# A two-layer graph network on one core: one gathered tile of each round fetched as 128 one-row DMAs

## The reference

```python
h = x @ W
e = leaky_relu(a_src[src] + a_dst[dst], NEG_SLOPE)      # layer 0, self loops included
m = segment_max(e, dst); e = exp(e - m[dst]); denom = segment_sum(e, dst)
out = segment_sum(h[src] * (e / (denom[dst] + 1e-16))[:, None], dst)
x = layernorm(x + tanh(out + bias))
...
h = gelu(x @ W_pre + b_pre)                              # layer 1
aggr = segment_sum(h[src] * edge_attr, dst)
y = gelu(gelu((x + aggr) @ W1 + b1) @ W2 + b2)
x = layernorm(x + (x + aggr) + y)
```

## Time and profile before

| | |
|---|---|
| median of 3 runs | 3728.23 us (3727.25 to 3732.05) |
| the profiled execution | 3727.72 us, its span 3725.9 us |
| busy: POOL, DVE, PE, ACT | 2784.2, 2436.9, 2399.7, 1285.1 us |
| gathers from the tables into `rows` (L699) | 2850, 946 ns each, some 0.30 us of idle before each |
| granted clock of PE | 0.5 in layer 0, 0.9 in layer 1 |

### The profile page before, as it was taken

How to read it: one execution, slowest core, us unless ns; L and a number is a source line. 1 busy time by engine, 2 the same in 40 slices (tenths; PEclk the granted TensorE clock), 3 DMA queues, 4 the chain that set the end, 5 groups by cost and what they waited for, 6 DMA issues and landing times.

```text
span 3725.9 us, 65212 instructions
## 1 busy us (share of the span) xinstructions
PE 2399.7 (64%) x16704; PEld 1951.8 (52%) x16705; DVE 2436.9 (65%) x6240; ACT 1285.1 (34%) x3893; POOL 2784.2 (75%) x2950
## 2 busy tenths in 40 slices
PE   6433343434344444444445989989988989999888
PEld 3333333333333333333334777777776777777776
DVE  7544444444466666566666777777777778888886
ACT  5433343434445555555553111111111122111222
POOL 7777777777777777777775777777777777777776
PEclk7555555555555555555556999999999999999998
DMA  5222222222222222222223343443434343444443
GB/s 101 44 42 42 42 44 42 44 42 43 42 44 43 44 43 44 43 44 45 44 44 101 90 94 90 95 94 93 95 91 95 92 96 91 97 97 96 92 96 70
DMA packets 336816, 254.46 MB, mean 68 GB/s; under 512 B 239277, under 2 KB 264370, under 8 KB 336539
## 3 DMA queue, kind: packets, MB, share of 16 engines
q0 software_dynamic: 94016, 146.16, 19.5%
q1 hardware_dynamic: 227905, 99.65, 11.4%
q10 hardware_dynamic: 14618, 6.14, 0.6%
HBM read 244.43 MB, written 7.25 MB: 68 GB/s over the span
## 4 chain that ended last, share of the span: by engine, by line
POOL 52%; issue 22%; PE 10%; DVE 6%; ACT 5%; DMA 2%; ACTq 1%; DVEq 1%; POOLq 0%; SPq 0%
POOL rows L699 52%; PE bank L1136 8%; ACT onehot L796 2%; PE bank L1123 2%; DMA rows<-table,src_i 2%; DVE hot L1555 1%; DVE score L1411 1%; ACT L839 1%; ACT pair L816 1%; ACTq L788 0%; DVEq L1326 0%; DVE cand L1376 0%; DVE newp L1402 0%; DVE cand L1375 0%; ACTq L827 0%
## 5 line engine op out<-in xcount | busy, mean ns | idle before, releaser
L699 POOL DMA_INDIRECT rows<-table,src_i x2850 | 2697.5, 946 | 896.4 <-issue 853.2
L1136 PE MATMUL bank<-node,hot 128*128 128x288 bf16 x9310 | 1231.2, 295 | 28.8 <-issue 14.5
L1045 PE MATMUL bank<-onehot,rows 128*97 128x72 f32 (+1 forms) x3048 | 584.9, 369 | 789.8 <-ACT onehot L826 789.8
L1136 PEld LDWEIGHTS bank<-node,hot 128*128 128x128 bf16 x9310 | 932.0, 101 | 285.5 <-issue 17.9
L1045 PEld LDWEIGHTS bank<-onehot,rows 128*97 128x97 f32 x3048 | 530.8, 281 | 829.2 <-issue 767.1
L1555 DVE TENSOR_SCALAR hot<-node,key 128x642 bf16<-128x642 int16 x1862 | 870.2, 538 | 110.7 <-PE bank L1136 58.4
L950 ACT ACTIVATE pair<-dst_i 128x8 f32 (+1 forms) x196 | 35.2, 180 | 1183.2 <-DVE rows L1581 921.6
L796 ACT ACTIVATE onehot<-iota,far_dst 128x72 f32 (+1 forms) x1564 | 384.3, 328 | 23.2 <-ACT far_dst L793 0.4
L1389 DVE SCALAR_TENSOR_TENSOR other<-onehot,bank 128x576 f32<-128x576 f32 (+1 forms) x196 | 121.6, 621 | 397.8 <-ACT bank L809 307.3
L1123 PE MATMUL bank<-onehot,rows 128*96 128x40 f32 (+1 forms) x3128 | 305.7, 255 | 85.9 <-DVE acc L1591 42.5
L1123 PEld LDWEIGHTS bank<-onehot,rows 128*96 128x96 f32 x3128 | 294.2, 169 | 108.8 <-issue 78.1
(11 more groups left out here) (204 smaller groups left out, 1972.3 us busy)
## 6 DMA issues: line engine op xcount, KB each, us to landing
attr<-in_edge_attr_dram SPq DMA_DIRECT2D x190, 336.0 KB
rows<-table,src_i POOLq DMA_INDIRECT x2850, 2.5
node<-in_src_dram SPq DMA_DIRECT2D x39, 320.0 KB
attr<-in_edge_attr_dram SPq DMA_DIRECT2D x190, 48.0 KB
table<-x SPq DMA_DIRECT2D x12, 196.0 KB
node<-table SPq DMA_DIRECT2D x8, 288.0 KB, 4.7
table<-rowt ACTq DMA_DIRECT2D x15, 144.0 KB
out_dram<-rowt ACTq DMA_DIRECT2D x15, 144.0 KB
```

The lines of the kernel that those rows point to most:

```text
L699: pool.indirect_dma_start(to, None, table, bass.IndirectOffsetOnAxis(ap=at, axis=0)).then_inc(landed, 16)
L1045: last = pe.matmul(total[:, 0:w], rows0(u, it)[:, j, 0:D1], wide(weights, w)[:, j, :], start=j == 0, stop=j == most - 1)
L1136: last = pe.matmul(p_got[t], hot[:, c % HOTS, i, t * P:(t + 1) * P], tab[:, a, :, :].rearrange("p k d -> p (k d)"), start=a == 0, stop=a = ...
```

## The change

In each of the rounds 1 to 38 of both layers the last group (u = 4, `rowed`) has one tile fewer to gather. Its 128 rows come one by one, each through a DMA of one row (392 bytes in layer 0, 384 in layer 1) into one partition of a new tile `single`. The byte offset of the row stands in a register, and the registers are loaded ten at a time from a line of offsets in SBUF (fetch_rows: one register load, then its DMAs). The offsets are made once at the start (two element-wise DMAs of `src`, two ACTIVATEs, a store to `row_at`) and loaded again for each round. In layer 0 SP issues 100 of the rows (44 as soon as `single` is free, 56 after e0.free has begun the round) and ACT 28, in three stops of 10, 10 and 8 behind the exponentials of the groups u = 0, 1 and 2. ACT copies the tile into `rows` and its last column to PSUM. In layer 1 SP issues 70, in portions of 14 behind its attribute DMAs, and ACT 58, in stops of 15, 15, 15 and 13 behind its feeds in the groups u = 0 to 3; DVE takes the product from `single` (multiplied_row) ahead of that of the gathered tiles. Work that reads `single` waits for all 128 rows; the first row of a round waits until `single` has been read.

```diff
+AT_ONCE = 10
+BY_SYNC0, AHEAD0 = 100, 44
+BY_SYNC1 = 70
...
-        def gathered(g, it):
+        def rowed(it, u):
+            return u == SLOTS - 1 and not first(it) and it is not ROUNDS
+        def row_bytes(eng, reg, table, n):
+            at = eng.snap(reg, True, min_val=0, max_val=(N - 1) * n * 4)
+            return table.rearrange("n d -> (n d)").bitcast(BYTE)[bass.ds(at, n * 4)].rearrange("(a b) -> a b", a=1)
+            return single[p:p + 1, 0:n].bitcast(BYTE)
+        def fetch_rows(eng, name, numbers, regs_at, table, n, first_row, landed):
+            for a in range(*regs_at, AT_ONCE):
+                b = min(a + AT_ONCE, regs_at[1])
+                regs = [eng.alloc_register(f"{name}{k}") for k in range(a, b)]
+                eng.load(regs, numbers[0:1, a:b])
+                for k, reg in enumerate(regs, a):
+                    eng.dma_start(row_place(first_row + k, n), row_bytes(eng, reg, table, n)).then_inc(landed, 16)
+        def gathered(g, it, u):
+            if u == SLOTS - 1:
+                return 16 * ((TILES - 1) * it + TILES)
             return 16 * (TILES * it + (LAST_T if g is LAST else TILES))
...
+            last_group = src[0:ROUNDS * SLOTS * GE].rearrange("(r e) -> r e", r=ROUNDS)[:, (SLOTS - 1) * GE:SLOTS * GE]
+            sp.dma_start(made_at[:, 0:P].rearrange("r (p j) -> r p j", j=1),
+                         last_group[:, 0:P * (TILES - 1)].rearrange("r (p j) -> r p j", j=TILES - 1)[:, :, TILES - 2:TILES - 1],
+                         allow_slow_non_contiguous=True).then_inc(s_last, 16)
+            sp.dma_start(made_at[:, P:2 * P].rearrange("r (p j) -> r p j", j=1),
+                         last_group.rearrange("r (p j) -> r p j", j=TILES)[:, :, TILES - 1:TILES],
+                         allow_slow_non_contiguous=True).then_inc(s_last, 16)
...
+            def row_numbers0(it):
+                sp.dma_start(sync_at[:, 0:BY_SYNC0], row_at[bass.ds(it, 1), P:P + BY_SYNC0]).then_inc(sync_at_in, 16)
+            def rows_begun0(it, name):
+                sp.wait_ge(sync_at_in, SYNC_AT0 + 16 * it)
+                sp.sem_inc(sync_go, 1)
+                sp.wait_ge(single_free, SINGLE0 + it - 1)
+                sp.sem_inc(sync_go, 1)
+                fetch_rows(sp, f"row0_{name}_", sync_at, (0, AHEAD0), table0, D2, 0, sync_row)
+            def rows_ended0(name):
+                fetch_rows(sp, f"row0_{name}_", sync_at, (AHEAD0, BY_SYNC0), table0, D2, 0, sync_row)
             def load0(it, k):
                 if not first(it):
                     sp.wait_ge(e0.free, (it + 1) * SLOTS)
                 if it is ROUNDS - 1:
+                    rows_ended0(it)
                     return
                 if first(it):
                     sp.wait_ge(e0.dst[0], 16)
                 round_of(dst_i, dst, it, 1 - k, e0.dst[0], 1)
                 if not first(it):
                     round_of(src_i, src, it, 1 - k, e0.src[0], 1)
+                    rows_ended0(it)
+                else:
+                    sp.wait_ge(a_st, 16 * CHUNKS)
+                    sp.wait_ge(act_at_in, 32)
+                row_numbers0(it + 1)
+                rows_begun0(it + 1, it)
             def load_round1(it, k):
                 near = TILES - 1
...
+            SHARE1 = -(-BY_SYNC1 // SLOTS)
+            PORTION1 = [(k * SHARE1, min((k + 1) * SHARE1, BY_SYNC1)) for k in range(SLOTS)]
+            AHEAD1 = 3
+            def fetch_rows1(it, portion, name):
+                if portion == 0:
+                    sp.wait_ge(sync_at_in, SYNC_AT1 + 16 * it)
+                    sp.sem_inc(sync_go, 1)
+                    sp.wait_ge(single_free, SINGLE1 + it - 1)
+                    sp.sem_inc(sync_go, 1)
+                fetch_rows(sp, f"row1_{name}_", sync_at, PORTION1[portion], table1, D, 0, sync_row)
+            def load_rows1(it, u):
+                if first(it):
+                    return
+                if u < AHEAD1 and not second(it):
+                    fetch_rows1(it - 1, SLOTS - AHEAD1 + u, it)
+                if u == AHEAD1 - 1:
+                    sp.dma_start(sync_at[:, 0:BY_SYNC1], row_at[bass.ds(it, 1), 0:BY_SYNC1]).then_inc(sync_at_in, 16)
+                if u >= AHEAD1:
+                    fetch_rows1(it, u - AHEAD1, it)
             def load1(it, k):
                 for u in range(SLOTS):
                     load_attr(it * SLOTS + u, it, u)
+                    load_rows1(it, u)
                     if u == 0 and not first(it):
                         load_booked_src(it)
                     if first(it) and u == SLOTS - 2:
...
-                    for j in range(TILES):
+                    for j in range(TILES - rowed(it, u)):
-                    for j in range(TILES - booked(it, u)):
+                    for j in range(TILES - booked(it, u) - rowed(it, u)):
...
+            act.wait_ge(s_last, 16 * 3)
+            act.activation(made_at[:, 0:P], made_at[:, 0:P], ACT.Copy, scale=float(D * 4))
+            act.activation(made_at[:, P:2 * P], made_at[:, P:2 * P], ACT.Copy, scale=float(D2 * 4)).then_inc(s_const, 1)
+            act.wait_ge(s_const, 6)
+            act.dma_start(row_at, made_at).then_inc(act_at_in, 16)
...
-                    act.wait_ge(e0.rows[u], gathered(g, it))
-                act.activation(p_src, rows0(u, it)[:, :, D1], ACT.Copy).then_inc(t0.given, 1)
+                    act.wait_ge(e0.rows[u], gathered(g, it, u))
+                t = TILES - rowed(it, u)
+                if rowed(it, u):
+                    act.wait_ge(sync_row, SYNC_ROW0 + 16 * BY_SYNC0 * it)
+                    act.wait_ge(act_row, ACT_ROW0 + 16 * (P - BY_SYNC0) * it)
+                    act.activation(rows0(u, it)[:, t, :], single[:, :], ACT.Copy)
+                    act.activation(p_src[:, t:TILES], single[:, D1:D2], ACT.Copy).then_inc(single_free, 1)
+                act.activation(p_src[:, 0:t], rows0(u, it)[:, 0:t, D1], ACT.Copy).then_inc(t0.given, 1)
+            def load_row_numbers0(it):
+                act.dma_start(act_at[:, 0:P - BY_SYNC0], row_at[bass.ds(it, 1), P + BY_SYNC0:2 * P]).then_inc(act_at_in, 16)
+            BY_ACT0 = (0, 10, 20, P - BY_SYNC0)
+            def fetch_rows0(it, part, name):
+                if part == 0:
+                    act.wait_ge(act_at_in, ACT_AT0 + 16 * it)
+                    act.sem_inc(act_go, 1)
+                    act.wait_ge(single_free, SINGLE0 + it - 1)
+                    act.sem_inc(act_go, 1)
+                fetch_rows(act, f"row0_{part}_{name}_", act_at, BY_ACT0[part:part + 2], table0, D2, BY_SYNC0, act_row)
+            def rows_along0(it, u):
+                if it is ROUNDS:
+                    return
+                if False:
+                    if u == SLOTS - 2 and it is not ROUNDS - 1:
+                        load_row_numbers0(it + 1)
+                    if u == SLOTS - 1 and it is not ROUNDS - 1:
+                        fetch_rows0(it + 1, 0, it)
+                    if u < 2 and not first(it):
+                        fetch_rows0(it, u + 1, it)
+                else:
+                    if u == SLOTS - 2 and it is not ROUNDS - 1:
+                        load_row_numbers0(it + 1)
+                    if u < 3 and not first(it):
+                        fetch_rows0(it, u, it)
             def weights(g, it, u, ws):
                 w = ws[0]
...
+                rows_along0(it, u)
                 if u == SLOTS - 1 and it is not ROUNDS - 1:
                     away(g + 2, it + 1, 1, ws[2])
             act.wait_ge(s_const, 5)
...
+                    if u == 0:
+                        load_row_numbers1(it)
+                    if u < SLOTS - 1:
+                        fetch_rows1(it, u)
+            BY_ACT1 = (0, 15, 30, 45, P - BY_SYNC1)
+            def load_row_numbers1(it):
+                act.dma_start(act_at[:, 0:P - BY_SYNC1], row_at[bass.ds(it, 1), BY_SYNC1:P]).then_inc(act_at_in, 16)
+            def fetch_rows1(it, part):
+                if part == 0:
+                    act.wait_ge(act_at_in, ACT_AT1 + 16 * it)
+                    act.sem_inc(act_go, 1)
+                    act.wait_ge(single_free, SINGLE1 + it - 1)
+                    act.sem_inc(act_go, 1)
+                fetch_rows(act, f"row1_{it}_", act_at, BY_ACT1[part:part + 2], table1, D, BY_SYNC1, act_row)
             def final_due(it):
...
+            def multiplied_row(it, u):
+                v.wait_ge(sync_row, SYNC_ROW1 + 16 * BY_SYNC1 * it)
+                v.wait_ge(act_row, ACT_ROW1 + 16 * (P - BY_SYNC1) * it)
+                at = slice((TILES - 2) * D, (TILES - 1) * D)
+                v.tensor_tensor(rows[:, u, at], single[:, 0:D], p_attr[:, at], ALU.mult).then_inc(single_free, 1)
             def multiplied_fetched(it, u):
                 v.wait_ge(g_out, it * 2 + (u > 0))
                         multiplied_fetched(it, u)
-                    multiplied(it, u, tiles_of(g) - booked(it, u)).then_inc(e1_msg, 1)
+                    if rowed(it, u):
+                        multiplied_row(it, u)
```

(1 more changed line is left out.)

27 lines of the change are left out of this document (24 added, 3 removed).

## The result

The changed kernel takes **4564.7 us** (median of 4 runs, 4560.2 to 4572.5) against 3729.0: a ratio of 1.224, interval 1.222 to 1.226, **836 us slower**. The forecast was 3972 and its range ended at 4220. The profiled execution has a span of 4562.2 us.

What follows compares the result with a forecast made beforehand. POOL, issuing a gather every 1.249 us, was taken to bound the kernel, with the other engines' chain close behind. The sum was 3727.7 + 164 (layer 0) + 77 (layer 1) + 3 (start) = 3972 us, range 3840 to 4220.

Steps and rivals of the forecast that it cites:

- c = 0.33 us: Time from issue to issue of one-row DMAs on SP and ACT: 0.33 us, bounds 0.30 and 0.38.
- Rival (2): Register-addressed issues are dearer (0.44 us), loads 0.6 us, and SP also bounds the narrow rounds: about 4465 us; chance 0.12.
- L = 0.4 us: Time of one register load ahead of ten row DMAs on SP or ACT: 0.4 us, bounds 0.28 and 0.6.
- ACT's way in layer 1: ACT's 58 rows between u = 0's message and u = 4's product: 31.2 us against 26.6 before, DVE waiting 4.6.
- ACT's addition of 11.5 us a round: Layer 0: queue time added to ACT each round by row DMAs, register loads, offsets DMA, ACTIVATEs, waits and marks: 11.5 us.
- Layer 0, wide, 53.3 and 62.1: Layer 0's wide rounds: 53.3 us without a middle, 62.1 with one; 1172 us against 999, +172.
- Narrow, 47.6 and hidden: Layer 0's narrow rounds: chain of 47.6 us stays under POOL's new 48.7, SP's 42.5 hidden; with middles, -8 us.
- Layer 1, wide, 43.65 and 50.35: Layer 1's wide rounds: 43.65 us without a final, 50.35 with one; 953 us against 874, +79.
- Landing 2.3 us: Time for a one-row DMA to land, taken from a small DMA: 2.3 us, bounds 2.0 and 2.5.
- The start, +3: Making the offsets table at the kernel's start costs +3 us, bounds 0 and 12.
- (1): Rival: the issues stay hidden, POOL sets the pace and the kernel is faster: 3633 us; chance 0.09.
- (3): Rival: layer 0 as forecast, layer 1 without lateness, so 47 us are gained there: 3847 us; chance 0.15.

Runs made afterwards that it cites:

- kernel with kept registers: Changed kernel, but each engine loads ten registers once and uses them for all its one-row DMAs, fetching the same ten rows repeatedly: 4061.4 us, ratio 1.0895.
- layer 1 alone: Changed kernel with the change in layer 1 only, the start's work kept, layer 0 gathering all its tiles on POOL: 4164.1 us.

## Why the prediction was wrong, point by point

The direction was right, and so was the mechanism on ACT, in both layers: stops of row DMAs on ACT move DVE. The size was not, because of the price of a register load, and with it one part of the mechanism fell: SP, which I had hidden, sets the pace of the narrow rounds of layer 0.

- **c = 0.33 us** from issue to issue: right (0.321 in a run, 0.33 and 0.35 on average on SP and ACT in layer 0), with some luck: I had no register instruction between the DMAs, the trace has a MOVE of 0.03 us ahead of each, and the DMA itself is 0.23, not 0.28. The estimate of 0.43 us from the Trainium skill ("DMA: Bandwidth & Descriptors", the section on why a DMA increments its semaphore by 16, with "Advanced Engine Details and Errata", Clock Domains) was too high; the trace has 0.23 for the instruction. Rival (2) put its weight on a dearer issue, and that part of it was false.
- **L = 0.4 us, bounds 0.28 and 0.6: the step that failed.** I took the price of a one-value load for one of ten and let the bound end at 0.6, with no row of a load of several values. It is 1.0 to 2.4 for ten. A round's loads are 17.4 us on SP in layer 0 (I had 4.4), 3.8 on ACT (1.2), and 12.9 on ACT in layer 1 (3.2). With these alone put into my own sum, SP is at 55.5 a round (measured 56.2) and becomes the bound of the narrow rounds, +99; the wide rounds give +225; ACT's way in layer 1 is 40.9 and gives 273 + 164 = +437. Together 3728 + 324 + 437 + 3 = 4492: 520 of the 593 us of error are this one term. The kernel with kept registers shows it from the other side, 503 us. But my sum isn't whole without the term either: with L = 0 it gives 3728 + 141 + 13 + 3 = 3885, and that kernel took 4061. Most of the 176 us are layer 1, where rows land late as soon as the loads no longer space them out.
- **ACT's addition of 11.5 us a round, layer 0:** measured 16.5 (58.3 - 41.8). Loads are 2.6 of the 5.0; the rest is there in the kernel without loads too (12.9 where my terms without L give 10.3). Some 0.5 is the longer step of ACT's issues; the other 1.9 lie in ACT's queue between the pieces of its stops, about 0.9 at the first of a round, which has its two waits and marks, and I do not split them further.
- **Layer 0, wide, 53.3 and 62.1:** measured 58.3 and 67.3 (medians of 7 and 11 rounds). **Narrow, 47.6 and hidden:** 56.1 on average, SP's cycle, which I had called hidden as long as c stays under 0.39; I had not named the same point for L, which is 0.4 + 6.2/11, about 0.96 us.
- **Layer 1, wide, 43.65 and 50.35:** 52.2 and 59.8. The wait at the product is there, ended by ACT's rows as forecast, but 7.6 us long; and ACT's feeds come late too (249 us, 6.5 a round), a wait that my count of ACT's way held but that I charged to nobody. The two together are 14.2 a round; my sum gives 14.3 with the real loads.
- **Landing 2.3 us:** too long where one queue is at work (1.2), and in the changed kernel's last step of layer 1 (1.3); too short where two issue without loads between (up to 6.4). That the slow loads keep the changed kernel from it is the likely reading, not one that a run isolates.
- **The start, +3:** layer 1 alone begins layer 1 at 1993.02, +2.8. Right.
- **Rivals.** (2), at 4465 and 0.12, came closest, and its picture is what happened: SP at 55.7 a round, ACT's way in layer 1 39.6 (measured 39.1). Only its cause was another, so that it came close was in part luck. (1) and (3) are out.

**Open:** what each queue costs apart and what the removed gathers would bring alone, on a chip without the stalls; where the stalls come from; whether SP's last portion is what lands late in layer 1 without loads, and what part the repeated addresses have in it; and why a load depends on where it begins.

## What to carry to other kernels

A price that the trace does not show needs a bound that allows for its kind, not one drawn close around the nearest row: ten values in one load are not one value, and the term stood 11 times in a round on one queue. Ask for each queue at which value of each unknown it becomes the bound, not only for the one unknown that you think of. And 128 one-row DMAs cost some 42 us of a queue (128 x 0.33) for what one gather does in 1.249; of the versions that ran where the kernel before takes 3729 us, the nearest, with the loads left out, took 9% more.
